# Six PSUM banks in one pool; ScalarE writes the first state of each half, times C, to the sums in place of VectorE

## The reference

```
c   = W[subject]^T x + b[subject]                      # per sequence, mixes the 64 tokens
m   = mamba(c)                                         # below
x1  = x + m
x2  = x1 W^T + adapter(x1)
out = x1 + sum_e cw[:, e] * swiglu_e(x2) + shared_swiglu(x2)

mamba:  xz = c @ in_proj^T;  x, z = split(xz)          # 1024 channels each
        xc = silu(conv of 4 taps(x))
        dt, B, C = split(xc @ x_proj^T)                # 128, 16, 16
        delta = softplus(dt @ dt_proj^T + bias)
        h_n[t] = h_n[t-1] * exp(delta * A_n) + delta * xc * B_n[t]     # 16 states n
        y = sum_n h_n * C_n[t];  y = (y + xc * D) * silu(z);  m = y @ out_proj^T
```

## Time and profile before

| | |
|---|---|
| median of 3 runs | 2017.18 us (2013.88 to 2018.59) |
| the profiled execution's own time | 2018.3 us |
| its span, first to last instruction | 2016.5 us |
| PE, PEld busy | 1707.2 us (85%), 1247.5 us (62%) |
| DVE, ACT, POOL busy | 1481.7 us (73%), 804.5 us (40%), 1054.7 us (52%) |
| mean granted TensorE clock | 0.904 of full speed |

### The profile page before, as it was taken

One profiled execution on the slowest core, in us unless ns is written; L12 is line 12 of the kernel. 1 busy time (PEld: TensorE's weight loads), 2 busy tenths in 40 slices (PEclk: granted clock), 3 DMA queues, 4 the chain that ended last, 5 costly groups with the idle time before them and its releaser, 6 DMA issues. The chain is left out here.

```text
span 2016.5 us, 28338 instructions
## 1 busy us (share of the span) xinstructions
PE 1707.2 (85%) x7908; PEld 1247.5 (62%) x7908; DVE 1481.7 (73%) x1981; ACT 804.5 (40%) x1190; POOL 1054.7 (52%) x823
## 2 busy tenths in 40 slices
PE   3857778598788888886867888999979999999998
PEld 2335444464445554445544454777869998999997
DVE  0379999999899999999999950567725566656564
ACT  0456556466566465564564421100012323323222
POOL 0069559787489595697886753000014443434343
PEclk9967988699898789996988879999989999999999
DMA  4212211222113222122222243211216665665664
GB/s 97 70 44 57 71 42 43 69 81 89 63 59 121 61 72 89 58 75 78 63 84 62 85 141 115 67 63 63 86 37 139 159 162 140 154 163 129 163 170 69
DMA packets 131940, 184.19 MB, mean 91 GB/s; under 512 B 23313, under 2 KB 81441, under 8 KB 128609
## 3 DMA queue, kind: packets, MB, share of 16 engines
q1 hardware_dynamic: 109200, 132.52, 20.6%
q0 software_dynamic: 17856, 44.85, 11.5%
q10 hardware_dynamic: 4720, 4.86, 0.9%
HBM read 277.64 MB, written 38.15 MB: 157 GB/s over the span
## 5 line engine op out<-in xcount | busy, mean ns | idle before, releaser
L1093 POOL TENSOR_TENSOR arena_kept<-arena_kept,b_all 128x512 f32<-128x512 f32 x512 | 638.0, 1277 | 251.1 <-DVE arena_kept L980 221.7
L980 DVE TENSOR_TENSOR_SCAN arena_kept<-da,arena_kept 128x512 f32<-128x512 f32 x512 | 597.7, 1205 | 36.8 <-ACT da L834 13.0
L631 PE MATMUL hT<-ident_kept,arena_kept 128*128 128x128 f32 x2048 | 329.7, 310 | 185.6 <-DVE yacc L998 111.9
L834 ACT ACTIVATE da<-arena_kept,a_neg 128x504 f32<-128x504 f32 x512 | 345.8, 684 | 318.4 <-DVE arena_kept L980 314.9
L631 PEld LDWEIGHTS hT<-ident_kept,arena_kept 128*128 128x128 f32 x2048 | 268.1, 159 | 298.7 <-DVE arena_kept L980 230.9
L998 DVE SCALAR_TENSOR_TENSOR yacc<-hT,c_now,yacc 128x512 f32<-128x512 f32 x480 | 333.4, 734 | 19.0 <-PE hT L631 17.9
L1997 POOL DMA_INDIRECT out<-y,slots_kept x76 | 132.1, 1738 | 268.5 <-issue 194.3
L478 PE MATMUL bank<-hid,wt 128*128 128x512 f32 x512 | 253.1, 643 | 6.4 <-ACT conv_sum L684 5.4
L478 PEld LDWEIGHTS bank<-hid,wt 128*128 128x128 f32 x512 | 102.4, 210 | 118.4 <-issue 109.4
L1633 POOL DMA_DIRECT2D slots_kept<-lists_kept x1 | 0.6, 568 | 252.2 <-DVE lists_kept L1583 252.2
L539 PE MATMUL bank<-skip,wt 128*128 128x512 f32 x256 | 126.7, 644 | 2.5 <-DVE skip L929 2.5
(11 more groups left out here) (218 smaller groups left out, 3181.6 us busy)
## 6 DMA issues: line engine op xcount, KB each, us to landing
w_up_kept<-in_up_T SPq DMA_DIRECT2D x76, 1408.0 KB, 6.1
w_dn_kept<-in_dn_T SPq DMA_DIRECT2D x76, 768.0 KB, 7.4
b_all<-bt_scratch SPq DMA_DIRECT2D x128, 256.0 KB, 3.6
wt<-in_in_T SPq DMA_DIRECT2D x64, 256.0 KB, 3.0
wt<-in_out_T SPq DMA_DIRECT2D x32, 256.0 KB, 3.0
x_in<-in_x_pad ACTq DMA_DIRECT2D x16, 256.0 KB
res<-in_x_pad SPq DMA_DIRECT2D x16, 256.0 KB, 4.1
x_scratch<-res SPq DMA_DIRECT2D x16, 256.0 KB, 2.0
```

The lines of the kernel that those rows point to most:

```text
L631: mm = nc.tensor.transpose(turned_in(j, m, t)[:, d * P:(d + 1) * P], h[:, m % RING, d, t * P:(t + 1) * P], ident[:])
L834: nc.scalar.activation(out[:, :, 1:], rows[:, :, 1:], ACT.Exp, scale=a_neg[:, d, n:n + 1]) \
L980: nc.vector.tensor_tensor_scan(h[:, n % RING, i, :], da[i % RING][:], dbx[:, i, :], 0.0, ALU.mult, ALU.add).then_inc(scan_done, 1)
L1093: nc.gpsimd.tensor_tensor(dbx[:, i, :], u[:, d, :], b_all[:, m % RING, :], ALU.mult) \
```

## The change

The two piece banks, the three `hT` banks and `conv_sum` become one pool of 6 banks. Which use gets which bank is worked out ahead by `banks_used`, which walks all pieces and turned states in TensorE's order. Each use gets the bank whose last use has the smallest `left`, a guess at the step at which that bank is emptied; a bank without a use counts as -1, and of equal ones the lowest number is taken. TensorE waits, use by use, for the emptying of the bank's last use. The pieces of `AHEAD` have the steps -27 to -1.

TensorE turns t = 0 to 3 without a piece between them. The last tap of the convolution and its sums are written in place to the `x` piece's own bank, which is free once VectorE has read it for the last time. The products of state 0 (`yacc[t] = hT * C_0`) move from VectorE to ScalarE: `first_state`, after each of the four decays of the step with n = 1. The code for shifted states, which was switched off, is gone.

```diff
-BANKS = 2
-TURNED = 3
+BANKS = 6
...
+def order_of(j, m):
+    pieces = [piece for piece in at_step(j, m) if name_and_number(piece)[0] in EMPTIED]
+    return pieces[:1] + list(range(TB)) + pieces[1:]
...
-    def __init__(self, uses, by_act):
-        self.by_act = by_act
-        self.bank = len(uses) % BANKS
-        self.last = uses[-BANKS] if len(uses) >= BANKS else None
-        uses.append(self)
+    def __init__(self, last_of, left):
+        self.bank = min(range(BANKS), key=lambda bank: last_of[bank].left if last_of[bank] else -1)
+        self.last = last_of[self.bank]
+        self.left = left
+        last_of[self.bank] = self
...
+def left_at(step, name, place):
+    if name == "h":
+        return step + (1.5 if place < RING else 2) if (step + 1) % NST else step + 1
+    if name == "x":
+        return step + 2
+    if name == "turn":
+        return step + (place + 2) / TB
+    if name in EMPTIED_BY_DVE:
+        return step + 1
+    return step + (1.4 if place == 0 else 1.9)
+
+SECTIONS = [("ahead", 0, [(m, AHEAD[m:m + 1]) for m in range(len(AHEAD))])]
...
+    for section, j, steps in SECTIONS:
+        for m, todo in steps:
+            step = j * STEPS + m - (len(AHEAD) if section == "ahead" else 0)
+            for place, piece in enumerate(todo):
+                if section == "body" and piece in range(TB):
+                    use = Use(last_of, left_at(step, "h", piece))
...
-    hT = [ps(f"hT{s}", [P, HT * P]) for s in range(TURNED)]
-    conv_sum = ps("conv_sum", [P, BLK])
...
+            def take(use):
+                last = use.last
+                if last is not None and last.kind == "h":
+                    pe.wait_ge(sum_done, last.place)
+                elif last is not None and last.kind == "first":
+                    pe.wait_ge(first_done, last.place)
+                elif last is not None and last.kind == "x":
+                    pe.wait_ge(conv_step, last.summed)
+                elif last is not None:
+                    pe.wait_ge(act_emptied if last.kind == "act" else dve_emptied, last.place + 1)
                 return banks[use.bank]
...
-                if section == "body" or e:
-                    act.wait_ge(conv_step, at.block * ((TAPS - 1) * DT) + (TAPS - 1) * e)
-                nc.scalar.mul(conv_sum[:], banks[at.bank][:], ch[:, e, W0 + TAPS - 1:W0 + TAPS]).then_inc(act_emptied, 1)
+                nc.scalar.mul(banks[at.bank][:], banks[at.bank][:], ch[:, e, W0 + TAPS - 1:W0 + TAPS]).then_inc(act_emptied, 1)
...
+            def first_state(j, m, t):
+                act.wait_ge(hT_full, j * SUMS + TB * m + t + 1)
+                act.wait_ge(c_copied, j + 1)
+                if m or j:
+                    act.wait_ge(bank_full, Place("body", j, "turn0" if m else "turn1").uses[-1].number + 1)
+                nc.scalar.mul(yacc[:, t, :], turned_in(j, m, t)[:], c_now[:, t, 0:1]).then_inc(first_done, 1)
...
                     for i in range(HT):
                         decay(j, *divmod(m, NST), i)
+                        if m % NST == 1:
+                            first_state(j, m - 1, i)
...
-                if n == 0:
-                    dve.wait_ge(c_copied, j + 1)
-                    nc.vector.tensor_scalar(yacc[:, t, :], turned_in(j, m, t)[:], scalar, None, ALU.mult).then_inc(sum_done, 1)
+                if n == 1:
+                    dve.wait_ge(first_done, firsts(j, m - 1, t))
...
                             for t in range(i - RING + 1, i + 1):
-                                add_state(j, g, n - 1, t)
+                                if n > 1:
+                                    add_state(j, g, n - 1, t)
```

More of the change, by code:

```diff
@@ L107, in filled @@
         self.place = emptied
[L110 to L116, removed]
-    full, emptied = 0, {True: 0, False: 0}
[L118 to L134, removed]
+def left_at(step, name, place):
[8 more added lines that the diff above has]
+    return step + (1.4 if place == 0 else 1.9)
@@ L191 @@
 STREAMED = {"x", "z", "out", "xa", "w"}
-STREAM = [(section, j, piece) for section, j, pieces in SECTIONS for piece in pieces
-          if name_and_number(piece)[0] in STREAMED]
+STREAM = [(section, j, piece) for section, j, steps in SECTIONS for _, todo in steps for piece in todo
+          if piece not in range(TB) and name_and_number(piece)[0] in STREAMED]
 TILE_OF = {use: n for n, use in enumerate(STREAM)}
@@ L448, in _ @@
         def _(pe):
[L449 to L453, removed]
+            def take(use):
[8 more added lines that the diff above has]
+                    pe.wait_ge(act_emptied if last.kind == "act" else dve_emptied, last.place + 1)
                 return banks[use.bank]
             def cond(at, c):
-                bank = take(at)
+                bank = take(at.uses[0])
                 pe.wait_ge(x_full, at.block * (32 * CONDS) + 32 * (c + 1))
@@ L520, in turn @@
             def turn(at, half):
-                pe.wait_ge(sum_done, sums_by_dve(at.block - 1, STEPS - 1, TB - 1) if half else sums_by_dve(at.block, NST - 1, TB - 1))
+                pe.wait_ge(sum_done, sums(at.block - 1, STEPS - 1, TB - 1) if half else sums(at.block, NST - 1, TB - 1))
                 for d in range(HT):
-                    bank = take(at, d)
+                    bank = take(at.uses[d])
                     for t in range(TB):
@@ L617, in piece_of, with turn_h @@
                     gate_logits(section, j, at)
-            def turn_h(j, m, tiles):
+            def turn_h(j, m, t):
                 pe.wait_ge(scan_done, j * SCANS + SCAN0 + HT * (m + 1))
[L622 to L633, removed]
+                bank = take(STATE_USES[j, m, t])
+                for d in range(HT):
+                    mm = nc.tensor.transpose(bank[:, d * P:(d + 1) * P], h[:, m % RING, d, t * P:(t + 1) * P], ident[:])
+                mm.then_inc(hT_full, 1)
             pe.wait_ge(const_in, 32)
@@ L1094, in inflow @@
                     .then_inc(dbx_made, 1)
-            def add_shifted(j, m, t):
-                pool.wait_ge(scaled[t], scaled_by_act(j, m))
-                nc.gpsimd.dma_start(out=yacc[:, t, :], in_=stage[:, SHIFTED.index(t), :], accum_op=ALU.add) \
-                    .then_inc(added[t], ADDED)
             pool.wait_ge(itok_in, 16)
```

125 lines of the change are left out of this document (61 added, 64 removed).

## The result

The changed kernel takes 2059.6 us (median of 4 runs, 2058.72 to 2061.59), the kernel before beside it 2016.83 us (2013.88 to 2018.59): a ratio of 1.0215, 95% interval 1.0197 to 1.0233. It is slower, 3.6 us above the forecast of 2056 and inside the range. The profiled execution took 2059.55 us, with a span of 2057.7.

A forecast was written before the change was run, and what follows sets the result against it. VectorE, busy 1002.7 of the steps' 1064 us, was taken to set the pace. The terms 43 - 5 + 14 - 10 - 3 = 39 us on 2018.3 gave 2057, as a median 2056 us; range 2038 to 2072.

The forecast's parts named there:

- one bank in turn for `x1` to `x7`: Ahead of the steps: every piece gets bank 0, so each tile waits 3.6 us for its release; 25 us in all.
- low clock in them: Ahead of the steps: each gap brings a stretch at 0.50, 1.7 us more a tile; 12 us, bounds 0 and 24.
- rest ahead of the steps: Behind the `x` tiles: `bc0`, `dt1` and `dt2` wait for banks, `dt3` ends 5.6 us later; 6 us, from 0 to 8.
- first states: Steps with n = 1: of 21 us of products leaving VectorE, ScalarE's queue leaves 5 us gained; bounds 0 and 21.
- ends of the first halves: Steps 15 and 16, blocks 0 to 2: states and `x` tiles wait for banks in use; 14 us lost, from 8 to 20.
- waits of TensorE that the pool saves: In the steps: 10 of VectorE's 17.9 us idle before adds behind TensorE go; bounds 0 and 25.
- end of the last block: `lg` no longer waits for row 2's bank, the last row's store is late next; 3 us gained, from 0 to 5.
- near 165: Sign of being right, ahead of the steps: the first scan starts near 165 us instead of 122.36.
- rival 2: Ahead of the steps: the `x` tiles run at the low clock throughout; 39 + 12, 2068 us; chance 0.15.
- nothing is left: Step 1 of blocks 1 and 2: ScalarE's later decays leave nothing of the gain from the moved products.
- in blocks 1 and 2 near 7: Sign of being right: steps of n = 1 take near 7 us in blocks 1 and 2, near 4.6 in block 3.
- Rival 3: Steps: banks held them back; products bring 21 us, waits go, half ends cost nothing, 31 us lost ahead; 1993 us; chance 0.05.

The follow-up runs named there:

- e4_filled_gaps: The changed kernel with three matmuls that nobody reads ahead of each of the tiles `x1` to `x7` of the first block; 2043.24 us, ratio 1.0132.
- e6_states_mended: The changed kernel with unused banks counting -100 and only the states of a half's last step leaving at step + 1.2; 1987.68 us, ratio 0.9857.
- e3_first_on_vector: e2_lefts_mended with the products of state 0 back on VectorE; 2000.67 us, ratio 0.9913.
- e2_lefts_mended: The changed kernel with unused banks at -100, a half's last states leaving at step + 1.2 and `x` tiles at step + 2.3; 1988.34 us, ratio 0.9851.
- e9_both_again: The same kernel as e2_lefts_mended, run again on another chip; 1990.56 us, ratio 0.9867.

## Why the prediction was right, and where its sizes were off

The time came out as forecast, and so did the mechanisms of the largest terms: the serial bank, the low clock behind its gaps and the ties at the ends of the halves. That the sum is within 2.1 us is in part luck, as shown below the table. The terms, in us on the profiled execution:

| step of the prediction | forecast | measured |
|---|---|---|
| one bank in turn for `x1` to `x7` | +25 | +27.2 |
| low clock in them | +12 (0 to 24) | +19.2 |
| rest ahead of the steps | +6 | +6.3 |
| first states | -5 | -4.2 |
| ends of the first halves | +14 | +14.2 |
| waits of TensorE that the pool saves | -10 | -13.8 |
| end of the last block | -3 | -3.8 |
| feed-forward | 0 | -4.0 |
| sum | +39 | +41.1 |

- **Ahead of the steps.** The planner's constant was read rightly: the first scan came at 175.1 us, forecast "near 165", and the difference is the clock's. Serial banks cost 27.2, not 25, since TensorE's tile of 3.70 us no longer overlaps with its neighbours (0.27 us a tile more than 3.43). Of the rest, TensorE waits 1.36 us before `bc` and 0.67 before `dt1` in the timeline after, forecast 1.4 and 0.6, and `dt2` waits for the copy out of `ct`, as forecast.
- **The clock is the term that was mis-sized.** The step that was off is "If each is followed by one such stretch, a tile takes 3.4 / 2 = 1.7 us more". It took the 3.4 us at 0.50 of the earlier trace rows as the price of any gap. For `x1` that was right to the tenth (5.40 - 3.70 = 1.7 us). For `x2` to `x7` the rows of after show 0.50 from before the tile's start through nearly all of it, at a price of 6.62 - 3.70 = 2.9 us each. e4_filled_gaps confirms the cause, and rival 2's upper bound of 24 was closer than the value taken. The Trainium skill (TensorE: Matmul & The Clock Gate, what is actually happening) calls throttled the default state which activity releases. The trace agrees for `x2` to `x7`, which begin at 0.50, and for e4_filled_gaps, where TensorE is kept busy and holds 1.00; `x1` began at 1.00 behind a gap as long. By that rule the prediction had the term "at 12 us or above", and 19.2 it was.
- **The ends of the halves.** Steps 15 to 17 of blocks 0 to 2 lost 14.2 us in sum, but in other shares: 2.5, 3.2 and 8.5 us, where the prediction had 1.7, 6 and 6. Step 15 of block 1 was slow before as well (14.8 us). The 0.7 us for `x7` behind `x6`'s convolution were 0.2 in e6_states_mended. In the sum 8.3 us after the adds' end "instead of 2.8" is 5.5, not 5.3. The match of 14.2 with 14 is closer than the mechanism deserves: 3.2 - 1.5 = 1.7 us of it are the clock at `xa` in blocks 2 and 1, 1.2 are step 17, which the prediction counts with the first states, and e4_filled_gaps, the same code in the steps, lost 17.7.
- **The first states.** ScalarE's queue took the gain, as forecast, and gave it back when its reads moved. In block 3 step 1 is 4.5 us and step 17 is 5.0. The 4.2 us are steps 1 of all blocks (-2.1) and step 17 of block 3 (-2.1); step 1 of block 1 grew by 1.2 us, where "nothing is left" was forecast. The sign "in blocks 1 and 2 near 7" missed for step 1: 8.3 us in both.
- **What the pool gives.** 13.8 us is what remains of the steps' stage when the other two terms are taken out, so it holds their errors too, and the 17 us more that first scans wait for the transposes, which no term had. e3_first_on_vector gives 16.3 us for the same with the guesses mended, `lg` included, and the forecast had 13.
- **End of the last block.** `lg` runs ahead of the copies and the store of the last row is what is late next, as forecast, in the kernel after:

```profile
1301.49 3.64 PE L609 MATMUL bank<-gate_T,x2T 128*128 128x16 f32 x32
...
1307.24 1.20 ACT L794 COPY x_sb<-bank 128x512 f32<-128x512 f32 x2 [5.79 <-DMA x_scratch<-x_sb]
1308.34 0.22 ACT L798 COPY logits_kept<-bank 128x64 f32<-128x64 f32 x1
```

The 3.8 us are no exact size either: from the last scan to the feed-forward it is 80.4 us after, and 77.4 in e4_filled_gaps with the same code there.

The overshoot of 7.2 us in the clock and 2.2 in the serial banks was masked by 3.8 us more from the pool and by 4.0 us from a stage that the change doesn't touch. On the medians the change cost 42.8 us, forecast 39.

Rival 3, the faster side, was wrong for this kernel, but the experiments show how far it reaches once its losses are taken out: 1988 us with the banks in order, and 1980 with ScalarE's order changed too, where the forecast of rival 3 was 1993 with 31 us still lost ahead of the steps. The Trainium skill (Trainium Kernel Development and Optimization, best practices) says that consistent bubbles can mean that SBUF or PSUM ran out. Here TensorE had 111.9 us of such bubbles, and the pool of six banks without its losses gave 16.3 us.

What stays open: why the clock at `xa` is low in some executions and not in others of the same kernel (step 15 of block 1 is 13.0 us in e2_lefts_mended, where VectorE waits 0.3 us for `xa`, 14.7 in e9_both_again with 2.0, and 16.1 in e3_first_on_vector with 3.4), why the transposes hold up more first scans with the pool, and how much of the last 8 us is the products' and how much the late reads'. The first products on ScalarE with the old banks weren't tried.

## What to carry to other kernels

A planner that ranks resources by a guess needs a value for "never used" below every guess that it can make, and its first decisions deserve a look in the order in which they fall: one constant cost 52 us here, more than the pool and the moved products together bring. Where an old use and a new one have the same guess, the planner must prefer the old one; a guess a fifth of a step later was worth 17 to 19 us. Work moved off the slowest engine is only worth its time if the engine that takes it has nothing queued ahead of what the slowest one waits for: the 32 products were worth 12 us, and together with two reads moved behind the decays 20.

## What the runs showed of the hardware

- The granted clock can fall out of step with the work. With 3.61 us of idle TensorE between tiles, 1.00 was granted from the end of a tile through most of the gap and 0.50 through nearly all of the next tile, tile after tile from `x2` on; a mean of 0.67 over 60 to 130 us, and 19.2 us lost in seven tiles that take 3.70 each at the full clock.
- Two executions of one kernel can get different clocks for the same work: the eight matmuls of `xa` in block 2 took 3.70 us at 1.00 in e2_lefts_mended and 6.55 at 0.52 in e9_both_again, and the slowest engine waited 2.9 us more for them.
- Matmuls that nobody reads paid for themselves: three in each gap brought the mean from 0.67 to 0.94 over 60 to 120 us and took 16.4 us off the kernel.
- ScalarE's last tap costs the same written in place to its own bank as to another one: 0.67 us at 84.51 in the timeline after, and 0.67 in the earlier trace rows.
